# The third value tile ahead of batch 1's queries in the first step of each layer

## The reference

```python
def _cross_attention(q_in, kv_in, wq, bq, wk, bk, wv, bv, wo, bo, bias_k, bias_v):
    qh = (q_in @ wq + bq).reshape(b, q_len, H, K)
    kh = (kv_in @ wk + bk).reshape(b, t, H, K)
    vh = (kv_in @ wv + bv).reshape(b, t, H, K)
    kh, vh = each with one learned row appended (bias_k, bias_v)
    weights = softmax(einsum('bqhk,bthk->bhqt', qh, kh) / sqrt(K))
    ctx = einsum('bhqt,bthk->bqhk', weights, vh).reshape(b, q_len, H * K)
    return ctx @ wo + bo

x = x + _cross_attention(layer_norm(x), xf, ...)     # layer 1
x = x + _cross_attention(layer_norm(x), xf, ...)     # layer 2
x = x + gelu(layer_norm(x) @ w_fc1 + b_fc1) @ w_fc2 + b_fc2
```

## Time and profile before

| what | value |
|---|---|
| median of 3 runs | 507.54 us (507.32 to 508.57) |
| profiled execution, its own time | 505.21 us |
| span of its trace | 503.4 us |
| mean granted TensorE clock | 0.999 |
| POOL busy | 414.2 us (82%) |
| DVE busy | 391.5 us (78%) |
| ACT busy | 331.8 us (66%) |

### The profile page before, as it was taken

How to read it: one execution, slowest core, us unless ns; L and a number is a source line. 1 busy time by engine, 2 the same in 40 slices (tenths; PEclk the granted TensorE clock), 3 DMA queues, 4 the chain that set the end, 5 groups by cost and what they waited for, 6 DMA issues and landing times.

```text
span 503.4 us, 11011 instructions
## 1 busy us (share of the span) xinstructions
PE 489.5 (97%) x3233; PEld 444.3 (88%) x3233; DVE 391.5 (78%) x910; ACT 331.8 (66%) x727; POOL 414.2 (82%) x387
## 2 busy tenths in 40 slices
PE   8998999999999999999999799999999999999897
PEld 5887998998999899999978699989989898999897
DVE  4887887888878878766779778788788788765795
ACT  3776866667767767675476677667676667678241
POOL 5876998989898998887497898989989898989632
PEclk9999999999999999999999999999999999999999
DMA  8436786656566675702115876676767575630001
GB/s 277 137 105 210 231 236 190 199 191 196 176 209 187 208 216 180 226 7 64 42 43 187 287 212 181 198 209 198 219 188 216 172 203 194 197 82 1 23 23 42
DMA packets 52741, 82.56 MB, mean 164 GB/s; under 512 B 5850, under 2 KB 33646, under 8 KB 52718
## 3 DMA queue, kind: packets, MB, share of 16 engines
q1 hardware_dynamic: 52718, 82.28, 53.6%
HBM read 53.42 MB, written 28.84 MB: 163 GB/s over the span
## 4 chain that ended last, share of the span: by engine, by line
PE 87%; DVE 4%; DMA 3%; POOL 2%; SPq 1%; issue 1%; ACT 1%; ACTq 0%; DVEq 0%; POOLq 0%
PE ring L1164 65%; PE acc L1164 10%; PE ps_ctx L1164 10%; DMA wf_lo<-spill 1%; DMA x_sb<-x_in 1%; PE ring L1210 1%; SPq L265 1%; DVE bn L922 1%; DVE k_lo L815 1%; DVE blocks L858 1%; DVE pT_lo L880 0%; POOL x_res L393 0%; ACT k_hi L556 0%; DVE z_sb L933 0%; DVE x_sb L914 0%
## 5 line engine op out<-in xcount | busy, mean ns | idle before, releaser
L895 DVE TENSOR_REDUCE row_max<-ring 128x1 f32<-128x512 f32 x112 | 76.4, 689 | 28.7 <-PE ring L1164 28.6
L624 ACT ACTIVATE probs<-ring,shift 128x512 f32<-128x512 f32 x112 | 76.4, 682 | 19.0 <-DVE shift L900 18.9
L406 POOL TENSOR_TENSOR v_lo<-v_sum,v_hi 128x512 fp32r<-128x512 f32 x64 | 82.9, 1298 | 0.0
L413 POOL TENSOR_SCALAR probs<-probs,inv 128x512 f32<-128x512 f32 x80 | 55.7, 701 | 29.2 <-DVE inv L908 29.1
L858 DVE STREAM_TRANSPOSE blocks<-probs 128x512 f32<-128x512 f32 x108 | 70.1, 687 | 1.5 <-POOL probs L413 1.1
L418 POOL TENSOR_TENSOR pT_lo<-wf_lo,pT_hi 128x1024 fp32r<-128x1024 f32 x28 | 67.1, 2417 | 0.0
L556 ACT ACTIVATE k_hi<-ring,cols 128x512 fp32r<-128x512 f32 x57 | 37.9, 689 | 35.2 <-PE ring L1164 35.1
L1164 PE MATMUL ring<-pT_lo,v_hi 128*128 128x256 f32 x208 | 58.4, 281 | 0.8 <-DVE pT_lo L880 0.8
L1164 PE MATMUL ring<-pT_hi,v_lo 128*128 128x256 f32 x208 | 58.0, 279 | 0.0
L1164 PE MATMUL ring<-pT_hi,v_hi 128*128 128x256 f32 x208 | 58.0, 279 | 0.0
L1164 PE MATMUL ring<-wv_lo,cT_hi 128*128 128x256 f32 x196 | 54.8, 279 | 0.0
(11 more groups left out here) (194 smaller groups left out, 1629.6 us busy)
## 6 DMA issues: line engine op xcount, KB each, us to landing
spill<-blocks SPq DMA_DIRECT2D x54, 512.0 KB, 2.8
wf_lo<-spill SPq DMA_DIRECT2D x112, 128.0 KB, 3.3
wf_hi<-spill SPq DMA_DIRECT2D x104, 128.0 KB, 3.2
wk_raw<-wk_in SPq DMA_DIRECT2D x17, 256.0 KB, 2.8
wq_raw<-wq_in SPq DMA_DIRECT2D x17, 256.0 KB, 3.5
wv_raw<-wv_in SPq DMA_DIRECT2D x16, 256.0 KB, 3.6
vrows<-vrows_in SPq DMA_DIRECT2D x16, 256.0 KB, 4.1
wo_raw<-wo_in SPq DMA_DIRECT2D x16, 256.0 KB, 2.7
```

The costliest lines, as they stand in the source:

```text
L406: pool.tensor_tensor(v_lo[:, 2 * m:2 * m + 2, :], v_sum[:, m % 2, :].rearrange("p (t c) -> p t c", c=PW), v_hi[:, 2 * m:2 * m + 2, :].bitc ...
L413: pool.tensor_scalar(probs[:, u, q, :], probs[:, u, q, :], inv[:, u, q:q + 1], 0.0, ALU.mult, ALU.add).then_inc(p_ready_pool, 1)
L624: act.activation(probs[:, u, q, :], ring[S_BANKS[where][QTB * u + q]][:], ACT.Exp, bias=shift[:, u, q:q + 1], scale=SCALE, accum_out=row_s ...
L895: dve.reduce_max(row_max[:, u, q:q + 1], ring[S_BANKS[where][QTB * u + q]][:], AX_X).then_inc(max_done, 1)
```

## The change

In the first step of each layer the third value tile (`project_v(2)`, with its sum on DVE, its rounding on ACT and its rest on POOL) is moved ahead of the queries of batch 1. The two heads of these queries get a bank each (ring4 and ring3) instead of half of ring4 each, and each head is rounded and split as soon as it is there, where before both were waited for. On ACT the two roundings move behind the exponentials of unit 1 and the rounding of the value tile; on POOL the rest of the value tile moves ahead of the split of `wq`. The banks of this step are dealt anew, and PE's waits with them.

```diff
-S_BANKS = {"first": [3, 1, 0, 5, 2, 0, 4, 3], ...
+S_BANKS = {"first": [3, 1, 0, 5, 1, 0, 4, 5], ...
...
-FIRST_Q_BANKS = [2, 4]
+FIRST_Q_BANKS = [[2, 2], [4, 3]]
...
# POOL, first_step
                 normalise(pair, 0, [0, 1])
+                value_rest(pair, 2)
                 next_wq(pair - 1, layer)
-                value_rest(pair, 2)
                 normalise(pair, 1, [1])
# ACT, round_first_q
-                act.wait_ge(q_filled, NQ * (pair + layer + b + 1))
+                act.wait_ge(q_filled, NQ * (pair + layer + 1) if b == 0 else NQ * (pair + layer + 1) + h + 1)
# ACT, first_step
                 exponential(pair, 0, 1, "first", layer, first=True)
-                round_first_q(pair, 0, 1, layer)
-                round_first_q(pair, 1, 1, layer)
                 exponential(pair, 1, 0, "first", layer, first=True)
                 exponential(pair, 1, 1, "first", layer, first=True)
                 round_v(pair, 2)
+                round_first_q(pair, 0, 1, layer)
+                round_first_q(pair, 1, 1, layer)
                 exponential(pair, 2, 0, "first", layer, first=True)
# DVE, first_step
                 shifts(pair, 1, 1)
+                sum_v(pair, 2, "first")
                 split_first_q(pair, 0, 1, layer)
                 split_first_q(pair, 1, 1, layer)
-                sum_v(pair, 2, "first")
# PE, first_step
                 scores(1, 1, "first")
+                project_v(2, "first")
                 pe.wait_ge(h_split_late, layer + 1)
                 project_first_q(0, 1, layer)
+                pe.wait_ge(exp_done, NS * pair + 1)
                 project_first_q(1, 1, layer)
-                pe.wait_ge(exp_done, NS * pair + 1)
-                project_v(2, "first")
                 pe.wait_ge(q_split, NQ * (pair + layer + 1) + 1)
+                pe.wait_ge(exp_done, NS * pair + 2)
                 scores(2, 0, "first")
...
-                pe.wait_ge(v_summed, NV * pair + 3)
+                pe.wait_ge(exp_done, NS * pair + 4)
                 scores(3, 1, "first")
...
                 project_q(1, "first")
+                pe.wait_ge(q_split, NQ * (pair + layer + 2) + 1)
+                project_k(1, "first")
                 pe.wait_ge(first_split, layer + 1)
-                project_k(1, "first")
+                project_k(2, "first")
                 pe.wait_ge(pT_split[0], pair - layer + 1)
-                project_k(2, "first")
-                pe.wait_ge(q_split, NQ * (pair + layer + 3))
                 project_k(3, "first")
```

More of the change, by code:

```diff
@@ L45 @@
 RUN = CTB * QTB * BLK
-S_BANKS = {"first": [3, 1, 0, 5, 2, 0, 4, 3], "step": [0, 1, 3, 4, 1, 2, 5, 0], "last": [0, 1, 3, 4, 2, 3, 4, 5]}
+S_BANKS = {"first": [3, 1, 0, 5, 1, 0, 4, 5], "step": [0, 1, 3, 4, 1, 2, 5, 0], "last": [0, 1, 3, 4, 2, 3, 4, 5]}
 C_BANKS = {"step": [2, 0, 2, 5], "last": [2, 1, 0, 2], "own": [4, 1, 3, 4]}
-V_BANKS = {"first": [None, None, 3, 0], "step": [5, 4, 0, 1], "last": [5, 0, 1, 3], "prologue": [3, 5], "between": [3, 0]}
-K_BANKS = {"first": [4, 1, 5, 3], "step": [1, 3, 2, 3], "last": [2, 2, 1, 5], "prologue": [5, 4, 0, 1]}
-FIRST_Q_BANKS = [2, 4]
-Q_BANKS = {"first": [2, 3], "step": [3, 4]}
-FIRST_PT_BANKS = [1, 5]
+V_BANKS = {"first": [None, None, 2, 0], "step": [5, 4, 0, 1], "last": [5, 0, 1, 3], "prologue": [3, 5], "between": [3, 0]}
+K_BANKS = {"first": [4, 1, 2, 3], "step": [1, 3, 2, 3], "last": [2, 2, 1, 5], "prologue": [5, 4, 0, 1]}
+FIRST_Q_BANKS = [[2, 2], [4, 3]]
+Q_BANKS = {"first": [1, 5], "step": [3, 4]}
+FIRST_PT_BANKS = [2, 3]
 PT_BANKS = [3, 1, 4, 0, 3, 0, 5, 0]
@@ L564, in round_first_q @@
             def round_first_q(pair, h, b, layer):
-                act.wait_ge(q_filled, NQ * (pair + layer + b + 1))
-                act.activation(q_hi[:, h, b * QLEN:(b + 1) * QLEN], ring[FIRST_Q_BANKS[b]][:, h * QLEN:(h + 1) * QLEN], ACT.Identity,
+                act.wait_ge(q_filled, NQ * (pair + layer + 1) if b == 0 else NQ * (pair + layer + 1) + h + 1)
+                act.activation(q_hi[:, h, b * QLEN:(b + 1) * QLEN], ring[FIRST_Q_BANKS[b][h]][:, h * QLEN:(h + 1) * QLEN], ACT.Identity,
                                bias=step_cols[:, pair, BQ, h:h + 1]).then_inc(q_rounded, 1)
@@ L826, in split_first_q @@
                 part = slice(b * QLEN, (b + 1) * QLEN)
-                dve.wait_ge(q_rounded, NQ * (pair + layer + b + 1))
-                dve.scalar_tensor_tensor(out=q_lo[:, h, part], in0=ring[FIRST_Q_BANKS[b]][:, h * QLEN:(h + 1) * QLEN],
+                dve.wait_ge(q_rounded, NQ * (pair + layer + 1) if b == 0 else NQ * (pair + layer + 1) + h + 1)
+                dve.scalar_tensor_tensor(out=q_lo[:, h, part], in0=ring[FIRST_Q_BANKS[b][h]][:, h * QLEN:(h + 1) * QLEN],
                                          scalar=step_cols[:, pair, BQ, h:h + 1],
@@ L1181, in project_first_q @@
             def project_first_q(h, b, layer):
-                queries(ring[FIRST_Q_BANKS[b]][:, h * QLEN:(h + 1) * QLEN], h, slice(b * QLEN, (b + 1) * QLEN)).then_inc(q_filled, 1)
+                queries(ring[FIRST_Q_BANKS[b][h]][:, h * QLEN:(h + 1) * QLEN], h, slice(b * QLEN, (b + 1) * QLEN)).then_inc(q_filled, 1)
             def project_v(m, where):
@@ L1320, in first_step @@
                 pe.wait_ge(p_ready_pool, NORMS_POOL * pair + 2)
-                pe.wait_ge(exp_done, NS * pair + 4)
                 transpose_first(1, layer)
@@ L1346, in step @@
                 scores(0, 1, "step")
+                pe.wait_ge(k_split, NK * pair + 3)
                 pe.wait_ge(v_split, NV * (pair - 1) + 2)
                 pe.wait_ge(pT_split[0], done)
-                pe.wait_ge(k_split, NK * pair + 3)
                 context(0, "step")
```

## The result

| what | before | changed |
|---|---|---|
| median of 13 runs | 507.21 us (504.76 to 508.57) | 510.02 us (507.60 to 511.56) |
| profiled execution, its own time | 505.21 us | 510.95 us |
| span of its trace | 503.4 us | 509.1 us |
| mean granted TensorE clock | 0.999 | 0.992 |

The ratio is 1.0062, 95% interval 1.0043 to 1.0082: 3.1 us slower by the ratio, 2.8 by the medians. 509.6 was forecast, from 2.1 us. The profiled execution is 5.7 us longer than that of before. So the sign was right, and the size needs an account of its own.

A forecast was written before the change was run, and what follows sets the result against it. PE, busy 97% of the span, was taken to bound the kernel, so breaks in its matmuls count. Delays of 1.07 us (layer 0) and 1.02 (layer 1) sum to 2.09, giving a median of 509.6 us, range 507.7 to 510.9.

The forecast's parts named there:

- The late `h_lo`: Layer 1, first step: the value tile fills PE's wait for POOL's `h_lo`, so the 1.12 us wait goes.
- Head 0's split, layer 0: ACT takes 1.94 us of other work before head 0's rounding, so `scores(2, 0)` starts 1.07 us late.
- The same in layer 1: `scores(2, 0)` of layer 1 starts 0.20 us late; the 1.12 us gained ahead are spent here.
- POOL's order, layer 1: `v_lo` ahead of `wq` takes 1.27 us against 0.3 slack, so `project_q(0, "first")` starts 1.02 us late, 0.20 included.
- The banks and the moved waits: First step: PE's new waits are for exponentials and splits that end early enough, so they cost nothing.
- The gate behind the first step: The exponential PE waits for hangs on its last key tile: it moves 1.07 and 1.02 us; waits of 1.8 and 2.7 stay.
- the 1.1 that was left open: Landing of unit 2, 3.10 us in layer 0 and 4.21 in layer 1: could vary 1.11 either way; no change taken.
- The sum: Both layers together: 1.07 + 1.02 = 2.09 us slower.
- The clock: New PE idle stretches of some 1.2 and 1.5 us cost nothing, since the clock stayed up behind a 2.70 us wait.
- The rival: Rival D: the clock falls behind the new idle stretches, 0.95 us each time, twice, giving 511.5 us; chance 0.03.
- The 2.33 us between the profiled execution and the median: Median of the runs stands 2.33 us above the profiled execution; added to its predicted 507.30 to give 509.63.

The follow-up runs named there:

- e2: The changed kernel with ACT's order as before (both heads' rounding ahead of the exponentials of unit 1), POOL still changed: median 510.82 us, ratio 1.0061 to the kernel before.
- e1: The changed kernel with POOL's order as before (split of `wq` ahead of the rest of the value tile): median 508.32 us, ratio 1.0013 to the kernel before.
- e4: The kernel before with POOL's new order alone (rest of the third value tile ahead of the split of `wq`): median 510.51 us, ratio 1.0063.
- e3: The changed kernel with both ACT's and POOL's order as before: median 507.17 us, ratio 0.9992 to the kernel before.
- e5: The changed kernel with SP reading unit 2 back before writing unit 3 in the first step: median 504.98 us, ratio 0.9958 to the kernel before.
- e6: The kernel before with SP reading unit 2 back before writing unit 3 in the first step: median 503.11 us, ratio 0.9915.
- e7: The changed kernel with the value tile in halves around the queries, queries earlier on ACT and DVE, POOL's order as before: median 506.60 us, ratio 0.9982 to before.

## Why the prediction was right, point by point

- *The late `h_lo` goes, worth 1.12.* Shown: no such wait in the changed kernel.
- *Head 0's split, layer 0, 1.07 late.* Measured 1.07. That ACT's order makes it is shown by e2, which takes 0.7 us from this wait and 1.1 from that of layer 1.
- *The same in layer 1, 0.20.* Measured 0.20.
- *POOL's order, layer 1, 1.02 with the 0.20 included.* Measured 3.98 - 3.02 = 0.96. e1 takes the wait away, and e4 makes one of its kind in the kernel before.
- *The banks and the moved waits cost nothing.* Shown by e3.
- *The gate behind the first step moves with PE.* Shown in its direction: the waits did not shrink by what PE comes late, they grew by 0.3 and 0.2 (2.12 and 2.89 against 1.83 and 2.70), and e5 and e6 show that they hang on SP's order. The landings were 0.5 and 0.2 us longer (3.57 and 4.39 against 3.10 and 4.21), within the 1.1 that was left open.
- *The sum, 2.09 us.* At equal clocks about 2, and 1.87 between e5 and e6, where the clock never falls. The 1.07 and 0.96 of the trace add up to 2.03.
- *The clock.* This step was wrong. "By the trace such a stretch costs nothing" was read off one execution in which the clock happened to stay up behind 2.70 us; in three of four runs of the kernel before (46 of 62) it falls, and e6 shows that these waits are the cause. The rival had the wrong place (the falls are not behind the new waits of 1.1 and 1.5 us but behind the old ones) and, at 0.03, too little weight. Its price of 0.95 was too small: 1.55 in the trace. The Trainium skill (TensorE: Matmul & The Clock Gate, "Part 1: The HAM clock gate"), against which I had put that one row, describes what the changed kernel's trace shows: half the clock behind an idle stretch (0.50 from 51 to 54), then the full one again. It shifts the median of both kernels, which is why it did little to the difference.
- *The 2.33 us between the profiled execution and the median.* I carried it along unexplained. 1.75 of it is one step of the clock (507.32 against 505.57), 0.36 the place of that execution among the runs at full clock (505.21 against 505.57), and 0.22 the small sample of three runs (507.54 against 507.32). Part of the spread at equal clocks is made at the program's start: PE is at the place of the change in layer 0 at 22.27 us in before's trace, at 21.87 in e2's and at 23.82 in e6's.
- *509.6 against 510.0.* That the number comes so close is in part luck: it stands on the median of three runs of before, 0.33 above that of 13, and it holds nothing for the clock, which was down longer in the changed kernel's runs.

What stays open is whether the change brings more time at the lower clock: 17 steps in 13 runs against 66 in 62. e2 and e4, which also wait longer in the first step, had 16 and 18 in 12; e3 and e7, with hardly a wait there, 10 and 12. But e1, with both waits for `q_lo`, had 11. Such counts differ by chance too, and no experiment set the frequency by itself.

## What to carry to other kernels

When a product is moved later on the engine that bounds, count what stands on the feeding engines' queues ahead of its conversion, from the first moment at which that queue can run: here ACT's 1.94 us of work ahead were in the rows, and so was POOL's slack of 0.3 us against the 1.27 that was put ahead. Before a difference of a few tenths of a per cent is explained, group the runs by their granted clock; a wait of 2 us on TensorE can cost 1.6 more behind it, and the largest gain in this kernel was to take that wait away by one change of order on the DMA queue.

## What the runs showed of the hardware that was not expected

Whether the clock falls is not set by the length of the idle stretch alone. In the profiled executions it fell behind 2.12, 2.18, 2.45, 2.66, 2.85, 2.89 and 3.22 us, and did not behind 1.75 to 1.98 (four times), nor behind 2.24 and 2.70 (twice). Nor does it fall at one fixed point: in the changed kernel's layer 0 the first two matmuls behind the wait still follow at 0.34 and 0.39 us and the low pace of 0.43 begins at 51.17, in e4 (layer 1, wait ending at 284.25) the first is already followed 0.60 us later. Nor are falls of one length: in the changed kernel 10 or 11 matmuls follow each other at the low pace, in e3 over 20, from 282.92 to 289.06, with PE busy all the time, and that fall cost 2.8 us (from 282.92 to the start of the next scores at 290.06, against 281.65 to 285.97 before). The same kernel has runs with no fall and runs with a mean clock of 0.993 or less.
